# Reordering the first stage of a graph layer: loads, low weights, mask forming and the normalization of second halves

## The reference, cut to what matters

```python
h = jnp.maximum(_layernorm(x, axis=-1), 0.0)
mask = (adj > 0)                                   # as float
deg = jnp.sum(mask, axis=1, keepdims=True)
agg = mask @ h / jnp.maximum(deg, 1.0)
combined = concatenate([h @ W_self + b_self, agg @ W_nb + b_nb])
out = x + relu(combined @ W_comb + b_comb)
```

## Time and profile before

| | us |
|---|---|
| median of 3 runs (lowest, highest) | 913.62 (911.9, 917.82) |
| the profiled execution's own time | 915.82 |
| its span, first to last instruction | 914.0 |
| stage 2's first product starts at | 120.02 |
| TensorE busy (share of the span) | 896.9 (98%) |
| VectorE busy | 799.1 (87%) |
| ScalarE, GpSimd busy | 377.5, 91.0 |

### The profile page before, as it was taken

The page is one execution under the profiler, slowest core; times in us unless marked ns, Lnnn a source line. Parts: engine busy times, 40 slices in busy tenths (PEclk is TensorE's granted clock), DMA queues, the critical chain, the costliest instruction groups (busy, mean ns, idle before and its releaser), DMA issues. The chain is left out here.

```text
span 914.0 us, 19105 instructions
## 1 busy us (share of the span) xinstructions
PE 896.9 (98%) x7720; PEld 760.1 (83%) x7720; DVE 799.1 (87%) x1512; ACT 377.5 (41%) x358; POOL 91.0 (10%) x132
## 2 busy tenths in 40 slices
PE   7999899899999999999999999999999999999997
PEld 5555478788888888888888888888888888888886
DVE  5999898898998988898889888888899998888884
ACT  3999854233333333332333333333333333333320
POOL 2888820000000000000000000000000000000000
PEclk9999999999999999999999999999999999999999
DMA  6467769999999999999999999999999999999950
GB/s 213 162 220 274 265 233 391 400 370 388 376 384 377 378 380 377 373 370 368 367 380 377 389 392 370 381 365 364 358 374 372 380 386 379 369 376 376 398 211 22
DMA packets 61367, 312.80 MB, mean 342 GB/s; under 512 B 6880, under 2 KB 8032, under 8 KB 28512
## 3 DMA queue, kind: packets, MB, share of 16 engines
q1 hardware_dynamic: 60736, 311.06, 87.7%
q10 hardware_dynamic: 544, 0.52, 0.2%
HBM read 294.78 MB, written 16.78 MB: 341 GB/s over the span
## 5 line engine op out<-in xcount | busy, mean ns | idle before, releaser
L625 PE MATMUL banks<-t,operands 128*128 128x257 f16 x7168 | 786.5, 272 | 2.6 <-DVE work L757 2.6
L625 PEld LDWEIGHTS banks<-t,operands 128*128 128x128 fp8e4 x7168 | 698.3, 97 | 90.7 <-issue 2.8
L468 ACT ACTIVATE mask<-stage,few 128x2048 fp8e4<-128x2048 int32 x128 | 252.7, 1999 | 415.5 <-DVE turned L720 318.9
L705 DVE TENSOR_SCALAR mask<-stage 128x2048 uint8<-128x2048 int32 x128 | 154.5, 1226 | 5.8 <-DMA stage<-in_adj_dram 5.8
L565 PE MATMUL banks<-t,xh 128*128 128x512 f16 x384 | 89.3, 383 | 4.2 <-DVE t L698 3.1
L757 DVE TENSOR_TENSOR work<-banks,work 128x512 f32<-128x512 f32 x32 | 22.1, 692 | 74.8 <-ACT work L518 74.8
L734 DVE TENSOR_TENSOR operands<-turned,operands 128x1024 uint32<-128x1024 uint32 x64 | 78.4, 1225 | 8.8 <-DVE turned L720 0.5
L714 DVE STREAM_TRANSPOSE operands<-mask 128x512 uint32<-128x512 uint32 x128 | 83.1, 687 | 0.2 <-DVE t L693 0.2
L720 DVE STREAM_TRANSPOSE turned<-mask 128x512 uint32<-128x512 uint32 x128 | 80.8, 669 | 0.0
L736 DVE TENSOR_TENSOR operands<-turned,operands 128x1024 uint32<-128x1024 uint32 x64 | 78.2, 1222 | 0.0
L565 PEld LDWEIGHTS banks<-t,xh 128*128 128x128 f16 x384 | 37.7, 98 | 44.0 <-issue 4.6
(11 more groups left out here) (62 smaller groups left out, 391.4 us busy)
## 6 DMA issues: line engine op xcount, KB each, us to landing
stage<-in_adj_dram SPq DMA_DIRECT2D x256, 1024.0 KB, 8.5
out_dram<-operands SPq DMA_DIRECT2D x32, 256.0 KB, 2.8
xh<-in_x_dram SPq DMA_DIRECT2D x32, 256.0 KB, 9.5
own<-out_dram SPq DMA_DIRECT2D x32, 256.0 KB, 10.5
out_dram<-xh SPq DMA_DIRECT2D x32, 256.0 KB, 6.0
t<-in_x_dram SPq DMA_DIRECT2D x30, 256.0 KB, 4.4
turned<-in_x_dram SPq DMA_DIRECT2D x2, 256.0 KB, 5.4
t<-in_L_gnn_W_nb_dram ACTq DMA_DIRECT2D x1, 256.0 KB, 4.0
```

The costliest lines, as they stand in the source:

```text
L468: act.activation(mask[:, b, :].bitcast(FP8), stage[:, b, :], ACT.Sigmoid, bias=steep, scale=STEEP, saturate=False).then_inc(formed_s, 1)
L625: mm = pe.matmul(banks[:, n, 0:width], bytes_of[:, c, :, s], t16[:, KQ * h + SUB * c + s, SLOT[n], 0:width], start=(h == 0 and c == 0 and ...
L705: dve.tensor_scalar(mask[:, b, :], stage[:, b, :], 0.0, float(MINUS_ONE_BYTE), ALU.is_gt, ALU.mult).then_inc(formed_v, 1)
```

## The change

The first loads are ordered anew: SyncE loads x pair 0, `W_self` and its half of `W_comb`, then the other pairs; the biases go to ScalarE's queue behind `W_nb`. The first batch of two pairs is split into two batches of one. In the opening, VectorE makes the second weight product's low half (`w_low(0)`) ahead of the statistics of pairs 2 and 3, GpSimd takes the four copies that widen the biases (`b_wide`), the negation of the weights' sum is cut in two, and the bias product on TensorE moves from behind `project(0)` to ahead of `turn(1)`. Four more warm-up transposes run.

The blocks of `adj` for step 0 are loaded at steps 0, 1, 3, 5 (before 12, 14, 16, 18), formed by ScalarE at steps 4 and 7 (before 20 and 22) and by VectorE at 9 and 13 (before 23 and 25), and transposed at 10 and 14. Step 1's blocks are loaded at steps 11 to 21; they are no longer formed in stage 1, and the two blocks of step 2 that were loaded there are loaded in stage 2. In stage 2 VectorE forms and transposes A22 and A11 of step 1 first, and `make_third(2)` stands ahead of `merge_a(0)`. From pair 3 on, second halves of odd pairs are normalized by VectorE, those of even pairs by GpSimd.

```diff
-WARM = 16
+WARM = 20
...
-BATCHES = [(0, 2), (2, 4), (4, 6), (6, 8)] + [(p, p + 4) for p in range(8, PAIRS, 4)]
+BATCHES = [(0, 1), (1, 2), (2, 4), (4, 6), (6, 8)] + [(p, p + 4) for p in range(8, PAIRS, 4)]
 STATS_AHEAD = {0: (6, 7), 1: (8, 9), 2: (10, 11)}
...
-FINISHED_AT = {(0, 2)[b - 3] if b < 5 else BATCHES[b][1] - 10: b for b in range(3, len(BATCHES))}
-SHIFTED_AT = {0: 2, **{j + 1: b for j, b in FINISHED_AT.items()}}
+FINISHED_AT = {(0, 2)[b - 4] if b < 6 else BATCHES[b][1] - 10: b for b in range(4, len(BATCHES))}
+SHIFTED_AT = {0: 3, **{j + 1: b for j, b in FINISHED_AT.items()}}
 BATCH_OF = {p: b for b, (first, end) in enumerate(BATCHES) for p in range(first, end)}
...
-FORM_STEPS_S = {20: A12, 22: A21}
-FORM_STEPS_V = {23: A22, 25: A11}
-TURN_STEPS_V = {24: A22, 26: A11}
+FORM_STEPS_S = {4: A12, 7: A21}
+FORM_STEPS_V = {9: A22, 13: A11}
+TURN_STEPS_V = {10: A22, 14: A11}
 TURN_STEPS = {30: (A12, A21)}
...
-NEXT_STEPS_V = {27: A22, 28: A11}
 X_AHEAD = 14
-LOAD_STEPS = {12: A12, 14: A21, 16: A22, 18: A11}
-NEXT_LOADS = {21: (1, A12), 23: (1, A21), 24: (1, A22), 26: (1, A11), 28: (2, A22), 29: (2, A11)}
+LOAD_STEPS = {0: A12, 1: A21, 3: A22, 5: A11}
+NEXT_LOADS = {11: (1, A22), 15: (1, A11), 18: (1, A12), 21: (1, A21)}
...
 def norms_v(j):
-    return (1,) if j < 3 else ()
+    return (1,) if j < 3 or j % 2 else ()
...
 def norms_g(j):
-    return () if j < 3 else (1,)
+    return () if j < 3 or j % 2 else (1,)
...
             load_x(0)
-            load_x(1)
             sp.dma_start(ws_t, w_self_t.rearrange("(h p) n -> p h n", p=P)).then_inc(w_loaded[0], DONE)
             sp.dma_start(wc[:, 0:HALVES, :], w_comb[0:D, :].rearrange("(h p) n -> p h n", p=P)).then_inc(w_loaded[0], DONE)
-            load_x(2)
-            load_x(3)
-            sp.dma_start(b_cols, b_cols_in[:, :]).then_inc(b_loaded, DONE)
-            sp.dma_start(bc_row, b_comb.rearrange("(a n) -> a n", a=1).partition_broadcast(P)).then_inc(b_loaded, DONE)
+            for j in range(1, 4):
+                load_x(j)
             for j in range(4, X_AHEAD):
...
             load_again(0)
-            load_block(2, A12)
-            load_block(2, A21)
+            load_step(2)
             load_step(3)
...
             root_of(0)
+            pool.wait_ge(b_loaded, 2 * DONE)
+            for m in range(2 * HALVES):
+                pool.tensor_copy(b_wide[:, m, :], b_cols[:, m:m + 1].to_broadcast([P, P])).then_inc(wide_ready, 1)
+            root_of(1)
+            pool.wait_ge(sum_high, 1)
+            pool.tensor_scalar(w12[:, 0, :, W_MINUS:W_WIDE], w12[:, 0, :, W_SUM:W_F1], -1.0, None, ALU.mult
+                               ).then_inc(sum_negated, 1)
             pool.wait_ge(sum_ready, 1)
-            pool.tensor_scalar(w12[:, :, :, W_MINUS:W_WIDE], w12[:, :, :, W_SUM:W_F1], -1.0, None, ALU.mult
+            pool.tensor_scalar(w12[:, 1, :, W_MINUS:W_WIDE], w12[:, 1, :, W_SUM:W_F1], -1.0, None, ALU.mult
                                ).then_inc(sum_negated, 1)
-            for b in range(1, 3):
+            for b in range(2, 4):
                 root_of(b)
...
                           ).then_inc(w_loaded[1], DONE)
+            act.dma_start(b_cols, b_cols_in[:, :]).then_inc(b_loaded, DONE)
+            act.dma_start(bc_row, b_comb.rearrange("(a n) -> a n", a=1).partition_broadcast(P)).then_inc(b_loaded, DONE)
...
             act.activation(rdeg[:, 0:1], steep, ACT.Sigmoid).then_inc(tables_ready, 1)
-            for j in range(2):
-                for t in norms_s(j):
-                    norm(j, t)
+            for t in norms_s(0):
+                norm(0, t)
             act.wait_ge(w_product, 1)
...
             high_of_h(0)
+            for t in norms_s(1):
+                norm(1, t)
             act.wait_ge(w_product, 2)
             w_high_half(0)
+            high_of_h(1)
             for t in norms_s(2):
...
             for j in range(PAIRS + 2):
-                if j + 1 < PAIRS:
+                if 1 <= j < PAIRS - 1:
                     high_of_h(j + 1)
...
                     pe.wait_ge(sum_ready, 1)
-                    pe.wait_ge(sum_negated, 1)
+                    pe.wait_ge(sum_negated, 2)
                 if j >= RING:
...
                 mm.then_inc(w_product, 1)
+                if j == 1:
+                    pe.wait_ge(wide_ready, 2 * HALVES)
+                    for m in range(2 * HALVES):
+                        mm = pe.matmul(pair_ps[2][:, 0, 0:D], b_wide[:, m, :], wc[:, m, :],
+                                       start=(m == 0), stop=(m == 2 * HALVES - 1))
+                    mm.then_inc(c_product, 1)
                 turn(j)
             project(0)
-            pe.wait_ge(wide_ready, 2 * HALVES)
-            for m in range(2 * HALVES):
-                mm = pe.matmul(pair_ps[2][:, 0, 0:D], b_wide[:, m, :], wc[:, m, :],
-                               start=(m == 0), stop=(m == 2 * HALVES - 1))
-            mm.then_inc(c_product, 1)
             turn(2)
...
-            for p in range(2):
-                stats_of(p)
+            stats_of(0)
             shifts(0)
-            for j in range(2):
-                for t in norms_v(j):
-                    norm(j, t)
+            for t in norms_v(0):
+                norm(0, t)
+            stats_of(1)
             dve.wait_ge(second_copied, 1)
...
             low_of_h(0)
-            for p in range(2, 4):
-                stats_of(p)
+            shifts(1)
+            for t in norms_v(1):
+                norm(1, t)
             w_low(0)
-            shifts(1)
+            stats_of(2)
+            stats_of(3)
+            low_of_h(1)
+            stats_of(4)
+            shifts(2)
             for t in norms_v(2):
                 norm(2, t)
-            dve.wait_ge(b_loaded, 2 * DONE)
-            for m in range(2 * HALVES):
-                dve.tensor_copy(b_wide[:, m, :], b_cols[:, m:m + 1].to_broadcast([P, P])).then_inc(wide_ready, 1)
-            for p in range(4, 6):
-                stats_of(p)
+            stats_of(5)
...
             for j in range(PAIRS + 3):
-                if j + 1 < PAIRS:
+                if 1 <= j < PAIRS - 1:
                     low_of_h(j + 1)
...
                     turn_own(0, TURN_STEPS_V[j])
-                if j in NEXT_STEPS_V:
-                    form(1, NEXT_STEPS_V[j])
                 if j in TURN_STEPS:
...
             dve.wait_ge(t_low, 2 * PAIRS)
-            make_second(1)
+            form(1, A22)
+            turn_own(1, A22)
+            form(1, A11)
+            turn_own(1, A11)
             make_third(1)
...
             make_second(2)
+            make_third(2)
             for r in range(PAIRS):
...
                 outer_sums(r)
-                if r == 0:
-                    make_third(2)
                 if i < STEPS:
```

## The result

| | before | after |
|---|---|---|
| median, lowest, highest | 913.5 (911.4 to 917.8), 9 runs | 919.5 (917.7 to 921.9), 9 runs |
| profiled execution, span | 915.82, 914.0 | 921.64, 919.8 |
| ratio, 95% interval | | 1.0063 [1.0045, 1.0080] |

The time lies in the range and within 1% of before, but it is 5 us above the forecast, and the interval excludes no change. In the comparisons with the experiments before ran another 86 times, with a mean granted clock of 0.9969; the changed kernel's nine runs have 0.9971. Straight lines through time against granted clock give 912.2 and 917.5 at full clock, 5.3 apart. So the difference is not made by the clock.

What follows compares the result with a forecast made beforehand. Stage 2 was taken as bound by TensorE, stage 1 by TensorE with VectorE close behind. Stage 2 starting 2.8 us later and -1.2 at the seam made +1.6 on the profiled 915.82; the median forecast was 914.5, range 908 to 920.

Steps and rivals of the forecast that it cites:

- Opening: Start of stage 1: `project(0)` at 15.2 and `project(1)` at 21.3, 1.4 us gained, between 0 and 2.0.
- Rival 4: Opening: low weights wait for the high ones on ScalarE, `project(0)` stays at 15.8; +1.4, 916 us; chance 0.1.
- Forms: Stage 1, early steps: 0.3 us of stall, 3.5 of VectorE's forms and transpositions, 0.5 of waits for GpSimd.
- Norms: Stage 1, odd pairs on VectorE: its step goes from 3.06 to 3.31 us, 3.9 us over 14 steps.
- Rival 3: Stage 1 norms: each waits a whole GpSimd instruction, taking 1.43 us rather than 0.61; +5.7, 920 us; chance 0.1.
- rival 1: Stage 1: VectorE keeps pace at 3.1 us a step, as GpSimd gets lighter; 910.4 us; chance 0.3.
- Tail: Stage 1 behind `project(23)`: nothing is lost any more, which gives back 3.9 us.
- First product: Start of stage 2: 2.8 us later than before, between 4 earlier and 6 later.
- Seam: From stage 1 to stage 2: a new 1.4 us wait on the merge, -1.2 us in sum, from -2.6 to +2.9.
- rival 2: Seam: `merge_a(0)` behind `make_third(2)`, blocks landing later, a wait of 5.5 us rather than 1.4; 918.6 us; chance 0.15.
- The old wait: Stage 2: before's 2.57 us wait, where the second merge stood on ScalarE behind late blocks' forms, was taken as 0.

Runs made afterwards that it cites:

- e2: The changed kernel with the norms put back, GpSimd normalizing all second halves from pair 3 on; ratio to before 1.0064.
- e3: The changed kernel with forms, block loads and stage 2's first VectorE instructions put back as before; new opening and norms stay; ratio to before 1.0008.
- e8: The changed kernel with `make_third(2)` put back behind `merge_a(0)` and `outer_sums(0)`; ratio to before 1.0054.
- e1: The kernel before with one edit: from pair 3 on, VectorE normalizes second halves of odd pairs; ratio to before 1.0019.
- e5: The kernel before with only ScalarE's two forms moved to steps 4 and 7, their loads to 0 and 1; ratio to before 1.0016.
- e4: The changed kernel with before's opening; early forms and new norms kept; ratio to before 1.0040.
- e7: The kernel before with ScalarE's forms at steps 5 and 14, their loads at 1 and 9; ratio to before 1.0006.
- e12: The kernel before with all four step 0 forms early, their loads and the new stage 2 start; norms on GpSimd, old opening; ratio to before 1.0047.
- e11: The kernel before with the new opening, x pair 1 loaded second, bias copies and product later, and ScalarE's forms at steps 5 and 14; ratio to before 1.0000.
- e9: The changed kernel with the bias product put back behind `project(0)`; ratio to before 1.0052.
- e10: The changed kernel with SyncE loading x pair 1 directly behind pair 0, as before; ratio to before 1.0051.
- e6: The kernel before with only VectorE's step 0 forms moved to steps 9 and 13, transpositions to 10 and 14; ratio to before 1.0012.

## Why the prediction was off by 5 us

Point by point, against the profiled times:

- **Opening: wrong.** "1.4 us gained"; `project(1)` began at 22.39, 0.3 earlier than before, where 21.3 was forecast, and 1.4 us were lost by `project(2)` (27.10; forecast 21.3 + 3.03 = 24.3), 1.7 of them by the clock. I gave GpSimd's late copies as the lower bound and didn't price x of pair 1 behind two more loads at all. But where that load landed earlier (e2, e3, e8), `w_low(0)` began at 14.3 to 14.6 and `project(0)` at 15.1 to 15.4, near the forecast (14.5 and 15.2), and the gain was gone by `project(2)` all the same (27.4, 25.3, 25.7). What failed in every profile of this opening is the way from `project(0)` to `project(2)`: `project(1)` took 4.44, 4.44 and 3.89 rather than 2.75 (changed kernel, e2, e8), in e2 behind a wait of 2.41 for GpSimd's norm, or TensorE waited 0.64 for that norm ahead of `project(2)` (e3). `project(0)` taking 2.75 was right, but not for my reason alone: with before's opening it took 2.75 in e1 and e5 as well. Rival 4, no gain in the opening, came true by another cause than its own. Over the profiles with before's opening (before, e1, e4 to e7, e12) `project(2)` lies between 24.8 and 25.7, over those with the changed one (after, e2, e3, e8) between 25.3 and 27.4.
- **Forms: mechanism right, size too small.** 0.3 + 3.5 + 0.5 = 4.3 forecast, 5.4 measured alone (e12) and 5.7 beside the new opening (e2). I counted VectorE's own time. What the timeline shows is that the lost lead exposes the chain of variances, root (2.03) and the norm behind them once for each batch, long after the forms.
- **Norms: too large.** VectorE's step was to rise by 0.25, to 3.31; alone it rose by 0.10 (e1), beside the forms the norms added 0.6 in all (e2; e4 against e12: 0.6 too), where 3.9 were forecast. The lock's price falls on the engine that waits, and with an instruction fewer for GpSimd that was mostly GpSimd: in the changed kernel's stretch of 62 to 101 us its norm takes 1120 ns and VectorE's low half 708. By the Trainium skill, "SBUF — State Buffer", section "SBUF: two separate sides", whichever of the two engines starts first has the shared ports for its whole instruction, and the other is blocked. This trace agrees: GpSimd's norm of 60.77 takes 0.55, and the one of 64.86, which starts with VectorE's two low halves, takes 1.58 and ends at 66.44, 0.43 behind the second of them. Rival 3, VectorE paying in full, did not happen. Of rival 1 the reason held in part (the relief pays for half, in the variances rather than in L693), its result did not.
- **`project(23)`** at 96.2 forecast, 97.09 measured. That is near for no good reason: +2.8 from the opening, +1.4 from the forms, -3.3 from the norms.
- **Tail: right.** 26.7 forecast, 26.8 measured, 3.8 given back.
- **First product**: 122.8 forecast, 123.91 measured.
- **Seam: right in place, mis-sized.** A wait on the first merge and none in the next group, as forecast, but 2.85 rather than 1.4: the blocks landed at 11.1, 14.3, 17.6 and 20.1 where I had 10.8, 13.3, 15.8 and 18.3. The loads went out at 6.1, 8.0, 8.3 and 9.6, near the 6, 8, 8.5 and 9 forecast, and the first took 5.0 to land, as forecast (4.8); 2.5 us a block, the full queue's rate, did not hold: 3.2, 3.3 and 2.5. That is part of rival 2. Its condition, A11 later than 17, can't tell it from the forecast, which had 18.3 itself. The old wait went as I took it. So the seam gave +0.3 rather than -1.2.
- **The stretch at 1.2 GHz** behind the wait, +1.6 in this profile, was in no term.

The time lies in the range by luck in part. Its upper end, 920, was set by rival 3, which did not happen, and the 919.5 lie between rivals 2 and 3 (918.6, 920) without the mechanism of either in full; the norms, forecast 3.3 too large, hide most of what the opening and the forms were too small.

The sum of errors on the profiled time: 1.1 + 1.5 + 1.6 = 4.2, and 917.4 was forecast for it where 921.64 was measured. For the median I had then gone down by another 0.7 (913.62 + 1.6 = 915.2 against 914.5), since my bounds reached further down; the runs gave no reason for it.

Open: at equal clock the change costs 5.3 us, while the first product and the wait together account for 4.2; some 1 us isn't placed. In e5, e7 and e11 the first product came 0.8 to 1.7 us earlier than in before, and in e9 and e10 1.9 and 2.4 earlier than in the changed kernel (0.5 and 1.0 earlier than in e8), without a measurable gain. Single runs of one kernel differ by up to 7 us, so one profile can't place 1 to 2 us in the median; the profiled executions of e2, e11 and e12 were the fastest of theirs, that of e6 the slowest. Neither GpSimd's norm ahead of the root in its queue, nor a split that gives VectorE the pair right behind each root, rather than odd ones, was tried; by e12's waits it is that norm that matters.

## What to carry to other kernels

Price a moved instruction by the lead it takes from the engine closest to the bound, and then ask which chain that lead was hiding: here it is a small root on a third engine, once a batch, and the loss goes on after the moved work is over. Then look whether the work that comes late needs that root or only stands behind it in the queue. Before moving a load, list what stands behind its waiter on that engine; here one load of 256 KB, two places later, was waited for 2.5 to 3.9 us. Before reading 1 us from a profile, find two kernels that are alike up to that point (here after and e8) and see how far they lie apart. When a wait moves to another place with about the same size (e8), that points to the late data as its cause, not the order.

## What the runs showed of the hardware that I had not expected

**The clock behind a wait.** In stage 2 TensorE, busy for 20 us and more, waited 2.4 to 3.9 us and went on. Sometimes it then ran for some 3.4 us at 1.2 GHz, and sometimes not. Windows of e8 and of e12, the 4 us around the end of such a wait (columns as above; the clock is the third number from the right):

```profile
174.00:178.00 4.00, 3.21 (x18) 2.40 (x19) 3.90 (x12) 0.19 (x1) 0.00 (x0) 0.57 1.03 423
```

```profile
148.00:152.00 4.00, 3.58 (x33) 3.21 (x34) 3.86 (x13) 0.24 (x1) 0.00 (x0) 1.00 1.01 404
```

Waits of 2.41, 2.43, 2.47, 2.48, 2.85, 2.88 and 3.32 had such a stretch behind them; those of 2.38, 2.55, 2.57 and 3.87, and the shorter ones of 0.97, 1.69 and 1.84, had none. The products' busy time shows the same: 786.5 us in before, e1, e2, e7 and e11, and 788.1 in the changed kernel, e3, e4, e5 and e10. So the length of the wait alone doesn't decide, and what does is open.

**The clock and the spread.** Over the runs of one kernel the time falls by about 0.8 us for each 0.001 of mean granted clock (86 runs of before, correlation -0.7; nine of the changed kernel, -0.94). At -0.7 that is about half of the variance of before's 912 to 919 us, and the spread is as large as what this change does.
